# Summing softmax denominators on GpSimd instead of TensorE in a decoder's first attention

## The chip, the cores and the metric

The kernel runs on one core of one Trainium2 chip. The metric is the device time of one execution in microseconds (us), the median of several runs. Each execution computes two whole decoder layers; the change touches only the first of the stages, the attention of layer 0.

## The reference

The input x is 4 x 512 x 512, float32. What the first stage computes, per batch of 512 tokens (the rest of the two layers follows and is untouched):

```python
def rotate_half(x):
    x1, x2 = jnp.split(x, 2, axis=-1)
    return jnp.concatenate([-x2, x1], axis=-1)
q, k, v = h @ Wq.T, h @ Wk.T, h @ Wv.T          # h = layernorm(x)
q = q * cos + rotate_half(q) * sin
k = k * cos + rotate_half(k) * sin
# 16 heads of 32 features
q_feat, k_feat = jax.nn.elu(q) + 1.0, jax.nn.elu(k) + 1.0
memory = jnp.einsum('bhsd,bhse->bhde', k_feat, v)
mem_out = (q_feat @ memory) / (q_feat . k_feat.sum(over keys))
attn = softmax(q @ k.T / sqrt(32)) @ v
combined = sigmoid(gate) * mem_out + (1 - sigmoid(gate)) * attn
x = x + combined @ Wo.T
```

The softmax needs, for each head and query, a sum of exponentials over the 512 keys. Who adds them up is what changes.

## The kernel before

The stage is `attention_linear`. Its tiles bear the prefix `a_` in the profile. A batch has four chunks of four heads (QUAD), so there are 16 steps g = 0 to 15; chunk order is (0, 2, 1, 3), and c = g mod 4. Each engine runs one program written out by hand over `STEPS`, a range from g = -3 to g = 16, and each step has eight slots s = 0 to 7 (PAIRS). Slot s stands for key tile t = s // 2 (128 keys) and pair of heads w = s % 2.

In a slot TensorE does, in this order: `scores_kq(g, s)`, the transposed scores of step g (keys on partitions, L1138); `scores_qk(g + 1, s)`, the scores of the next step whose row maxima are wanted (L1120); then a half of the weighting, two slots late. `half(g, n)` is `weigh(g, t)` for even n (values times exponentials, L1150, into bank NUM) and `add_up(g, t)` for odd n (a matrix of ones times the same exponentials, L1158, into bank SUMS). Each half is four matmuls on 32 columns each of the array. So values and sums alternate, and both accumulate over the four key tiles in their banks. ScalarE turns each pair of kq banks into exponentials (L1268) in `probs`, which holds two key tiles of four heads.

Six PSUM banks rotate as three pairs, numbered by the order of `place` (the dictionary `turn`). `claim` makes TensorE wait until the pair used three places before has been drained. Hence `scores_qk(g + 1, s)` waits for the exponentials of slot s - 1, and what follows slot 7 of an even step (`values`, or `outputs`) gets the pair of kq slot 7 and waits for that slot's exponentials.

Other work rides along. In an even step the rotation of steps g + 2 and g + 3 is made: `rotate_first`, `rotate_second` and `rotate_third` on VectorE (L1387, L1390, L1394), and on GpSimd L1505 (`rot1`), L1506 (`mul3`), `low(g + 2)` (L1483) and L1510 (`rot2`). In an odd step GpSimd has `low(g + 2)` alone, and after `normalise` two `linear` (L1497). `normalise(g - 1)` (L1487 and L1492) writes `oT`, which the output product of a batch needs. At c = 2 TensorE computes `values` of the next batch at slot 0 and after slot 7; at odd steps it has the matmuls of the linear memory (L1172, L1181, L1182, L1190) and two `project` after slot 7 (L59 to L61); at c = 0 `outputs` (L1225) stands after slot 7 and needs `normalise(g - 1)`; at c = 1 it stands at slots 1, 3 and 5, each followed by VectorE's `add_residual` (L1413) and a store and a load of `res` on the SP queue. ScalarE's `maxima_rows` issues two DMAs that put the maxima beside the operands of the next step's kq scores.

The SP queue carries `stack(g)`, 12 DMAs each (L1073), and the residual's. `cosT` and `sinT` hold both rotated chunks (two of 128 rows) for the whole stage.

## Time and profile before

| | |
|---|---|
| time, median of 3 runs | 3030.02 us (3027.96 to 3043.7) |
| the profiled execution: span, first to last instruction | 3028.2 us (the median lies 1.8 us above it) |
| the stage of the change, by its instructions | about 20 us to 666 us of the span |
| PE busy, whole span | 2476.7 us (82%) |
| DVE, ACT, POOL busy, whole span | 1884.0, 1239.5, 851.9 us |
| exponentials of the stage (L1268) | 128 instructions, 130.8 us |

PE is TensorE, DVE is VectorE, ACT is ScalarE, POOL is GpSimd, SP is SyncE with its DMA queue. In the views, x counts instructions; a float32 matmul appears as two instructions, so four matmuls of a half read x8. Timelines give start, duration, engine, line, operation and tiles, and in brackets the idle time before and who ended it. PEclk is the granted TensorE clock, 1.00 for 2.4 GHz and 0.50 for 1.2 GHz.

### The profile page before, as it was taken

What the parts mean: (1) busy time and instruction counts of PE and PEld (TensorE: products, weight loads), DVE (VectorE), ACT (ScalarE), POOL (GpSimd) and SP (SyncE); (2) the same over time, 40 slices, a digit from 0 to 9 for tenths busy, and PEclk for the clock granted to TensorE, in tenths of its full rate; (3) what the DMA queues carried; (4) which work ended last, traced back from release to release, by engine and by line L of the source; (5) the groups of instructions that cost most, each with busy time, mean ns of one, the idle gap of its engine ahead of it and who ended that gap; (6) DMA issues with size and microseconds to landing.
All of it is one profiled execution on the core that took longest, in us unless ns stands there. A gap on an engine that the chain in (4) does not pass through costs nothing. (4 is left out here: it accounts for less than half of the span.)

```text
span 3028.2 us, 35090 instructions
## 1 busy us (share of the span) xinstructions
PE 2476.7 (82%) x12822; PEld 1644.7 (54%) x12822; DVE 1884.0 (62%) x2959; ACT 1239.5 (41%) x1873; POOL 851.9 (28%) x1176
## 2 busy tenths in 40 slices
PE   5898989864443357999448999999999879999999
PEld 4454545321222237998334554545555538888887
DVE  3766575627899985778557777565655444444443
ACT  2444444428656625666103433334333323333332
POOL 2232222215657634555343332001211110000000
PEclk8999999976665678999768999999999979999999
DMA  3213132212222346988585655334433423101000
GB/s 117 65 43 84 43 84 46 70 61 77 77 80 77 108 163 213 308 300 289 158 185 136 159 146 157 88 89 104 109 95 91 115 80 127 42 0 42 1 28 15
DMA packets 186940, 323.55 MB, mean 107 GB/s; under 512 B 20450, under 2 KB 52066, under 8 KB 186788
## 3 DMA queue, kind: packets, MB, share of 16 engines
q1 hardware_dynamic: 168356, 270.44, 30.0%
q0 software_dynamic: 15360, 50.34, 6.3%
q8 instruction: 88, 1.44, 0.2%
q10 hardware_dynamic: 3072, 0.79, 0.1%
q14 instruction: 64, 0.52, 0.1%
HBM read 182.30 MB, written 62.92 MB: 81 GB/s over the span
## 5 line engine op out<-in xcount | busy, mean ns | idle before, releaser
L757 DVE TENSOR_REDUCE at_negmax<-at_ps 128x2 f32<-128x1024 f32 (+3 forms) x256 | 259.1, 1016 | 120.3 <-PE at_ps L523 63.1
L670 ACT ACTIVATE at_probs<-at_ps 128x1024 f32<-128x1024 f32 (+3 forms) x256 | 221.7, 866 | 267.4 <-PE at_ps L538 263.3
L1367 DVE TENSOR_REDUCE a_negmax<-a_ps 128x2 f32<-128x1024 f32 x128 | 155.2, 1217 | 136.4 <-PE a_ps L1120 135.8
L59 PE MATMUL ff_ps<-ff_xnT_hi,ff_s_hi 128*128 128x512 f32 x512 | 200.8, 392 | 5.1 <-DVE ff_xnT_lo L2878 5.1
L60 PE MATMUL ff_ps<-ff_xnT_lo,ff_s_hi 128*128 128x512 f32 x512 | 200.1, 391 | 0.0
L61 PE MATMUL ff_ps<-ff_xnT_hi,ff_s_lo 128*128 128x512 f32 x512 | 200.1, 391 | 0.0
L1946 ACT ACTIVATE gr_act_signs<-gr_signed,gr_test 128x512 bf16<-128x512 f32 x248 | 177.4, 717 | 42.3 <-POOL gr_test L2339 20.4
L2908 DVE TENSOR_TENSOR ff_hid<-ff_hid,ff_ps 128x512 f32<-128x512 f32 x64 | 44.0, 688 | 238.6 <-ACT ff_hid L2853 238.6
L538 PE MATMUL at_ps<-at_qk 98*128 98x512 f32 (+3 forms) x512 | 171.7, 417 | 21.0 <-DMA at_qk<-at_mrow 10.6
L1268 ACT ACTIVATE a_probs<-a_ps 128x1024 f32<-128x1024 f32 x128 | 130.8, 1023 | 135.2 <-PE a_ps L1138 134.6
L518 PE MATMUL at_ps<-at_qk 96*128 96x512 f32 (+3 forms) x512 | 162.9, 382 | 19.0 <-DVE at_xnT_lo L818 8.9
L538 PEld LDWEIGHTS at_ps<-at_qk 98*128 98x128 f32 x512 | 83.3, 194 | 162.5 <-issue 93.6
L2853 ACT ACTIVATE ff_hid<-ff_ps 128x512 f32<-128x512 f32 x64 | 38.3, 598 | 303.3 <-PE ff_ps L61 303.3
L59 PE MATMUL ex_ps<-ex_x_hi,ex_gu_hi 128*128 128x256 f32 x512 | 148.4, 290 | 6.3 <-issue 5.8
L60 PE MATMUL ex_ps<-ex_x_lo,ex_gu_hi 128*128 128x256 f32 x512 | 145.7, 285 | 0.0
L61 PE MATMUL ex_ps<-ex_x_hi,ex_gu_lo 128*128 128x256 f32 x512 | 145.6, 284 | 0.0
L852 POOL TENSOR_SCALAR_AFFINE_SELECT at_probs<-at_probs 128x256 f32<-128x256 f32 x128 | 52.4, 411 | 291.4 <-ACT at_probs L670 291.4
L782 DVE RECIPROCAL at_weighed<-at_weighed 128x128 f32<-128x128 f32 x128 | 119.7, 939 | 15.2 <-ACT at_weighed L705 15.2
L2635 POOL TENSOR_TENSOR ex_d_lo<-first_d,ex_d_hi 128x1024 fp32r<-128x1024 f32 x32 | 87.4, 2730 | 136.5 <-ACT ex_d_hi L2561 136.4
L873 POOL TENSOR_TENSOR at_oT<-at_weighed 128x512 f32<-128x512 f32 x32 | 40.7, 1270 | 296.6 <-DVE at_weighed L782 296.6
L726 ACT CAST at_part<-at_ps 128x512 fp32r<-128x512 f32 x64 | 37.4, 587 | 211.7 <-PE at_ps L61 200.7
L630 PE MATMUL at_ps<-at_wo,at_oT 128*128 128x512 f32 x256 | 115.9, 607 | 6.8 <-POOL at_oT L873 6.6
(431 smaller groups left out, 6640.1 us busy)
## 6 DMA issues: line engine op xcount, KB each, us to landing
at_qk<-at_part SPq DMA_DIRECT2D x384, 128.0 KB
first_gu<-in_L_ffn_w_gate_up_dram SPq DMA_DIRECT2D x32, 1024.0 KB, 13.4
a_qk<-a_part SPq DMA_DIRECT2D x192, 128.0 KB
first_d<-in_L_ffn_w_down_dram SPq DMA_DIRECT2D x32, 512.0 KB, 13.6
out_rows<-ex_y SPq DMA_DIRECT2D x32, 512.0 KB
gr_aside_raw<-in_L_ffn_W_dram SPq DMA_DIRECT2D x48, 256.0 KB, 3.1
w13T<-gr_aside_out SPq DMA_DIRECT2D x32, 256.0 KB, 3.2
shared_x<-x_after_cross SPq DMA_DIRECT2D x8, 1024.0 KB
```

What stands on the lines that cost most here:

```text
L59: pe.matmul(out, lh, rh, start=start, stop=False, skip_group_check=True)
L60: pe.matmul(out, lh, rl, start=False, stop=False, skip_group_check=True)
L61: return pe.matmul(out, ll, rh, start=False, stop=stop, skip_group_check=True)
L518: mm = pe.matmul(bank(key, i, 0, n), qk[0:KROWS, g % STACKS, 0, j, t * P:(t + 1) * P], qk[0:KROWS, g % STACKS, 1, j, 0:n], start=True, sto ...
L538: mm = pe.matmul(bank(key, i, lo), qk[0:KROWS + 2, g % STACKS, 1, j, t * P:(t + 1) * P], qk[0:KROWS + 2, g % STACKS, 0, j, lo:S], start=Tr ...
L630: mm = pe.matmul(bank(key, i), oT[:, dc, t * P:(t + 1) * P], woT[:, dc, :], start=dc == 0, stop=dc == NC - 1, skip_group_check=True)
L670: act.activation(probs[:, t % 2, 2 * w:2 * w + 2, lo:S], banks(("kq", g, s), lo), ACT.Exp, scale=SCALE).then_inc(free(("kq", g, s)), 1)
L757: dve.reduce_max(negmax[:, g % 2, :].rearrange("p (j t) -> p j t", t=NT)[:, 2 * w:2 * w + 2, t], banks(("qk", g, s), 0, width(g, t)), AX.X ...
L782: dve.reciprocal(weighed[:, 1, t * P:(t + 1) * P], weighed[:, 1, t * P:(t + 1) * P]).then_inc(rec_done, 1)
L1268: act.activation(probs[:, t % 2, 2 * w:2 * w + 2, :], banks(("kq", g, s)), ACT.Exp, scale=SCALE).then_inc(free(("kq", g, s)), 1)
L1367: dve.reduce_max(negmax[:, g % 2, :].rearrange("p (j t) -> p j t", t=NT)[:, 2 * w:2 * w + 2, t], banks(("qk", g, s)), AX.X, negate=True).t ...
L1946: act.activation(act_signs[:, j, :], src, ACT.Sign, scale=-1.0, bias=against, accum_out=total[:, i, j:j + 1]).then_inc(counted_to[j], 1)
```

## The change

TensorE no longer runs `add_up` for each key tile. GpSimd adds the exponentials of key tiles 1, 2 and 3 onto those of tile 0, in place, with six additions of 128 x 1024 per step (`fold`, three for each pair of heads), and `add_up(g)` then runs once per step, in slot 1 of the next step. `probs` becomes five half tiles (a half is one key tile and one pair of heads, 128 x 1024): three are used in turn for w = 0, two for w = 1. Tile 0's half must now stay until the sum is taken, so for w = 1 the tiles 1, 2 and 3 all use the same half. The exponentials wait for the values' matmuls and the fold that last read their half. `cosT` and `sinT` hold one chunk each and are loaded anew in odd steps by `load_tables`, after `stack`, 256 KB a table; the gate's load gets a semaphore of its own.

```diff
-        probs = sb("probs", [P, 2, QUAD, S])
+        probs = sb("probs", [P, 5, 2, S])
-        cosT, sinT = sb("cosT", [P, NC // 2, S]), sb("sinT", [P, NC // 2, S])
+        cosT, sinT = sb("cosT", [P, 1, S]), sb("sinT", [P, 1, S])
...
+        def at_half(g, t, w):
+            if w == 0:
+                return ((0, 1, 2, 1)[t] - g) % 3
+            return 3 + (g + (t > 0)) % 2
+
+        def probs_of(g, t, j):
+            return probs[:, at_half(g, t, j // 2), j % 2, :]
+
+        def both_of(g, t, w):
+            return probs[:, at_half(g, t, w)]
...
         @block.sync
         def _(sp):
+            def load_tables(n):
+                if n:
+                    sp.wait_ge(const_in, 32 * n)
+                    sp.wait_ge(mul1, 2 * n)
+                    sp.wait_ge(mul2, n)
+                    sp.wait_ge(mul3, n)
+                for dst, src in ((cosT, env.cos), (sinT, env.sin)):
+                    sp.dma_start(dst[:], src.rearrange("(c p) s -> c p s", p=P)[n % 2].rearrange("p (o s) -> p o s", o=1)).then_inc(const_in, 16)
...
                 if has(g + 2):
                     stack(g + 2)
+                if g % 2 and g >= -1 and has(g + 3):
+                    load_tables((g + 3) // 2)
...
-            def add_up(g, t):
-                if t == 0 and g >= 1:
+            def add_up(g):
+                if g >= 1:
                     pe.wait_ge(sums_out, g)
+                for w in range(2):
+                    pe.wait_ge(folded[w], (NT - 1) * (g + 1))
                 for j in range(QUAD):
-                    mm = pe.matmul(ps[j * HD:(j + 1) * HD, SUMS, :], ones[:], probs[:, t % 2, j, :],
-                                   start=t == 0, stop=t == NT - 1, skip_group_check=True)
+                    mm = pe.matmul(ps[j * HD:(j + 1) * HD, SUMS, :], ones[:], probs_of(g, 0, j), start=True, stop=True, skip_group_check=True)
                 mm.then_inc(sums_done, 1)
 
             def half(g, n):
                 if n % 2 == 0:
                     weigh(g, n // 2)
-                else:
-                    add_up(g, n // 2)
+                elif n == PAIRS - 1:
+                    add_up(g)
...
                 act.wait_ge(kq_ready, PAIRS * g + s + 1)
-                if NT * g + t >= 2:
-                    act.wait_ge(sums_done, NT * g + t - 1)
-                act.activation(probs[:, t % 2, 2 * w:2 * w + 2, :], banks(("kq", g, s)), ACT.Exp, scale=SCALE
-                               ).then_inc(free(("kq", g, s)), 1)
+                if t == 0 and g:
+                    act.wait_ge(values_done, NT * g - (1, 0)[w])
+                    act.wait_ge(folded[w], (NT - 1) * g - (1, 0)[w])
+                if t == 1 and g:
+                    act.wait_ge(sums_done, g)
+                if t == 3 or (t, w) == (2, 1):
+                    old = t - 2 + w
+                    act.wait_ge(values_done, NT * g + old + 1)
+                    act.wait_ge(folded[w], (NT - 1) * g + old)
+                act.activation(both_of(g, t, w), banks(("kq", g, s)), ACT.Exp, scale=SCALE).then_inc(free(("kq", g, s)), 1)
...
         @block.gpsimd
         def _(pool):
+            def fold(g, t, w):
+                wait_drained(pool, "kq", g, 2 * t + w)
+                if t == 1:
+                    wait_drained(pool, "kq", g, w)
+                    pool.wait_ge(values_done, NT * g + 1)
+                else:
+                    pool.wait_ge(folded[w], (NT - 1) * g + t - 1)
+                pool.tensor_tensor(both_of(g, 0, w), both_of(g, 0, w), both_of(g, t, w), ALU.add).then_inc(folded[w], 1)
+
+            def fold_tile(g, t):
+                for w in range(2):
+                    fold(g, t, w)
...
+                own = has(g)
                 if g % 2 == 0 and has(g + 2):
                     pool.wait_ge(mul1, g + 4)
                     pool.tensor_tensor(turn1[:], turn1[:], turn2[:], ALU.subtract).then_inc(rot1, 1)
-                    pool.tensor_tensor(raw[1][:], raw[1][:], table(cosT, g + 2), ALU.mult).then_inc(mul3, 1)
+                    pool.tensor_tensor(raw[1][:], raw[1][:], table(cosT), ALU.mult).then_inc(mul3, 1)
+                    if own:
+                        fold_tile(g, 1)
                     low(g + 2)
                     pool.wait_ge(mul2, g // 2 + 2)
                     pool.wait_ge(mul3, g // 2 + 2)
                     pool.tensor_tensor(raw[1][:], raw[1][:], turn2[:], ALU.add).then_inc(rot2, 1)
-                if g % 2 and has(g + 2):
+                elif g % 2 and has(g + 2):
                     low(g + 2)
+                    if own:
+                        fold_tile(g, 1)
+                elif own:
+                    fold_tile(g, 1)
+                if own:
+                    fold_tile(g, 2)
+                    fold_tile(g, 3)
                 if has(g - 1):
                     normalise(g - 1)
```

The order on GpSimd in an even step with rotation (here g = 2), before: L1505 and L1506 are `rot1` and `mul3`, L1483 is `low`, L1510 `rot2`, L1487 and L1492 `normalise(g - 1)`, and then comes `low` of step 3.

```order
L1505 TENSOR_TENSOR a_turn<-a_turn 128x1024
L1506 TENSOR_TENSOR a_raw<-a_raw,a_cosT 128x1024
L1483 TENSOR_TENSOR a_part<-a_turn,a_part 128x2x512
L1510 TENSOR_TENSOR a_raw<-a_raw,a_turn 128x1024
L1487 TENSOR_TENSOR a_weighed<-a_weighed 128x512
L1492 TENSOR_TENSOR a_oT<-a_weighed,a_lin 128x512
```

The same place in the changed kernel (L1547, L1548, L1524, L1554, L1528 and L1533 are the same operations, L1516 is a fold):

```order
L1547 TENSOR_TENSOR a_turn<-a_turn 128x1024
L1548 TENSOR_TENSOR a_raw<-a_raw,a_cosT 128x1024
L1516 TENSOR_TENSOR a_probs<-a_probs 128x1024 x2
L1524 TENSOR_TENSOR a_part<-a_turn,a_part 128x2x512
L1554 TENSOR_TENSOR a_raw<-a_raw,a_turn 128x1024
L1516 TENSOR_TENSOR a_probs<-a_probs 128x1024 x4
L1528 TENSOR_TENSOR a_weighed<-a_weighed 128x512
L1533 TENSOR_TENSOR a_oT<-a_weighed,a_lin 128x512
```

Two folds now stand ahead of `low`, four between `rot2` and `normalise`.

ScalarE over the slots 4 to 7 of an even step of the changed kernel (g = 0), with the semaphores that each instruction waits on (L1297 is the exponentials, L1313 and L1318 belong to the feature map, L1327 are the DMAs of the maxima):

```order
L1297 ACTIVATE a_probs<-a_ps 128x1024 [waits a0_kq_ready]
L1313 ACTIVATE a_raw<-a_turn 128x1024 [waits a0_mul2,a0_rot1]
L1297 ACTIVATE a_probs<-a_ps 128x1024 [waits a0_folded1,a0_values_done,a0_kq_ready]
L1318 ACTIVATE a_turn<-a_turn 128x1024 [waits a0_feat_exp,a0_p_lo]
L1297 ACTIVATE a_probs<-a_ps 128x1024 [waits a0_folded0,a0_values_done,a0_kq_ready]
L1297 ACTIVATE a_probs<-a_ps 128x1024 [waits a0_folded1,a0_values_done,a0_kq_ready]
L1327 DMA a_qk<-a_mrow 1x16x128 [waits a0_w_turned]
```

Before, each of these exponentials waited on `sums_done` and `kq_ready`; those of slots 5, 6 and 7 now wait on folds and on the values' matmuls.

## Rows read from the trace of the kernel before

**Rows 1.** Busy time, steps 2 to 5: stretch, length, PE, PEld, DVE, ACT, POOL, PEclk, DMA.

```profile
165.70:194.64 28.94, 28.42 (x147) 15.51 (x145) 19.48 (x18) 15.29 (x16) 11.80 (x6) 1.00 0.24 56
194.64:231.87 37.23, 36.32 (x194) 21.65 (x193) 22.39 (x27) 16.34 (x20) 8.67 (x6) 1.00 0.19 44
231.87:260.23 28.36, 23.03 (x107) 8.74 (x105) 23.12 (x31) 14.25 (x15) 14.80 (x7) 0.88 0.38 103
260.23:313.37 53.14, 49.74 (x235) 27.82 (x234) 30.66 (x37) 17.25 (x21) 7.47 (x5) 1.00 0.24 65
```

**Rows 2.** Timeline of PE, step 6: in slots 1 and 2, then at its end.

```profile
322.02 1.07 PE L1158 MATMUL a_ps<-a_probs,a_ones 128*32 128x512 f32 x8
323.02 0.73 PE L1138 MATMUL a_ps<-a_qk 98*128 98x512 f32 x2
...
336.72 0.28 PE L1127 MATMUL a_ps<-ident,a_negmax 128*16 128x128 f32 x1 [0.33 <-DVE a_negmax L1367]
342.34 0.62 PE L1138 MATMUL a_ps<-a_qk 98*128 98x512 f32 x2
```

**Rows 3.** Timeline of POOL, step 6.

```profile
324.57 2.37 POOL L1505 TENSOR_TENSOR a_turn<-a_turn 128x1024 f32<-128x1024 f32 x1 [16.87 <-DVE a_turn L1390]
326.89 2.39 POOL L1506 TENSOR_TENSOR a_raw<-a_raw,a_cosT 128x1024 f32<-128x1024 f32 x1
329.24 3.37 POOL L1483 TENSOR_TENSOR a_part<-a_turn,a_part 128x1024 fp32r<-128x1024 f32 x1
332.57 2.38 POOL L1510 TENSOR_TENSOR a_raw<-a_raw,a_turn 128x1024 f32<-128x1024 f32 x1
```

**Rows 4.** Timeline of ACT, step 6: the exponentials of slot 7.

```profile
334.92 1.02 ACT L1268 ACTIVATE a_probs<-a_ps 128x1024 f32<-128x1024 f32 x1 [0.31 <-PE a_ps L1138]
```

**Rows 5.** Timeline of DVE, step 6: the second and the third rotation product.

```profile
323.27 1.22 DVE L1390 TENSOR_TENSOR a_turn<-a_raw,a_sinT 128x1024 f32<-128x1024 f32 x1
...
327.53 2.84 DVE L1394 TENSOR_TENSOR a_turn<-a_raw,a_sinT 128x1024 f32<-128x1024 f32 x1
```

**Rows 6.** Busy PE in stretches around the end of step 0: PEclk, DMA.

```profile
118.00:120.00 2.00, 0.00 (x0) 0.85 0.87 199
120.00:122.00 2.00, 1.28 (x3) 0.50 0.59 133
...
126.00:128.00 2.00, 2.00 (x13) 0.95 0.00 0
```

**Rows 7.** Timeline of POOL, step 4: its first row and its `normalise`.

```profile
237.71 2.38 POOL L1505 TENSOR_TENSOR a_turn<-a_turn 128x1024 f32<-128x1024 f32 x1 [11.53 <-DVE a_turn L1390]
...
251.39 1.26 POOL L1487 TENSOR_TENSOR a_weighed<-a_weighed 128x512 f32<-128x512 f32 x1 [3.28 <-DVE a_weighed L1380]
252.73 2.13 POOL L1492 TENSOR_TENSOR a_oT<-a_weighed,a_lin 128x512 f32<-128x512 f32 x1
```

**Rows 8.** Timeline of PE at the end of step 4: the output product.

```profile
254.91 5.88 PE L1225 MATMUL a_ps<-a_wo,a_oT 128*128 128x512 f32 x8 [4.12 <-POOL a_oT L1492]
```

**Rows 9.** Timeline of POOL, step 0: its first row.

```profile
104.19 2.38 POOL L1505 TENSOR_TENSOR a_turn<-a_turn 128x1024 f32<-128x1024 f32 x1 [10.44 <-DVE a_turn L1390]
```

**Rows 10.** Timeline of PE: first matmul of step 1.

```profile
120.21 1.22 PE L1138 MATMUL a_ps<-a_qk 98*128 98x512 f32 x2 [3.61 <-DMA a_qk<-a_mrow]
```

**Rows 11.** Timeline of ACT, step 15: the maxima's DMAs, the exponentials of slot 2.

```profile
616.05 1.15 ACTq L1299 DMA_DIRECT2D a_qk<-a_mrow  x2
...
625.31 1.02 ACT L1268 ACTIVATE a_probs<-a_ps 128x1024 f32<-128x1024 f32 x1
```

**Rows 12.** Timeline of PE, step 15: its first matmul, the last product with ones.

```profile
618.51 1.22 PE L1138 MATMUL a_ps<-a_qk 98*128 98x512 f32 x2 [3.46 <-DMA a_qk<-a_mrow]
...
635.57 1.04 PE L1158 MATMUL a_ps<-a_probs,a_ones 128*32 128x512 f32 x8
```

**Rows 13.** Timeline of SP's queue, step 5: one `stack`.

```profile
266.87 8.45 SPq L1073 DMA_DIRECT2D a_qk<-a_part  x12
```

**Rows 14.** Timeline of DVE, step 5: a residual addition.

```profile
280.56 0.69 DVE L1413 TENSOR_TENSOR a_res<-a_ps,a_res 128x512 f32<-128x512 f32 x1 [2.47 <-DMA a_res<-in_x_dram]
```

More of the change, by code:

```diff
@@ L981, in linear_unit, with table @@
             return m if g % 2 and s >= first and (s - first) % 3 == 0 and has(m) else None
-        def table(which, m):
-            c = chunk(m)
-            return which[:, c:c + 1, :].to_broadcast([P, 2, S])
+        def table(which):
+            return which[:].to_broadcast([P, 2, S])
+        def at_half(g, t, w):
[6 more added lines that the diff above has]
+            return probs[:, at_half(g, t, w)]
         def reciprocal_parts(g, s):
@@ L1040, in attention_linear @@
         stack_in, mx_in = [sem(f"stack_in{i}") for i in range(STACKS)], sem("mx_in")
-        res_in, res_out, const_in = sem("res_in"), sem("res_out"), sem("const_in")
+        res_in, res_out, gate_in, const_in = sem("res_in"), sem("res_out"), sem("gate_in"), sem("const_in")
+        folded = [sem(f"folded{w}") for w in range(2)]
         ones_set, rows_set, gates = sem("ones_set"), sem("rows_set"), sem("gates")
@@ L1061, in _ @@
         def _(sp):
[L1062 to L1064 removed]
+            def load_tables(n):
[6 more added lines that the diff above has]
+                    sp.dma_start(dst[:], src.rearrange("(c p) s -> c p s", p=P)[n % 2].rearrange("p (o s) -> p o s", o=1)).then_inc(const_in, 16)
+            load_tables(0)
+            sp.dma_start(gate_e[:], gate.rearrange("a h b c -> (a b c h)").partition_broadcast(P)).then_inc(gate_in, 16)
             def stack(g):
@@ L1382, in rotate_first @@
             def rotate_first(m):
-                dve.wait_ge(const_in, 16 * 3)
+                dve.wait_ge(const_in, 32 * (m // 2 + 1))
                 wait_drained(dve, "p", m + 1)
```

15 lines of the change are left out of this document (6 added, 9 removed).

## The prediction

> **What bounds the kernel now.** I read the stage step by step, since the share of busy time over the whole span says nothing of it. The busy time of the steps [rows 1] shows TensorE working 28.42 of 28.94 us in step 2, 36.32 of 37.23 in step 3 and 49.74 of 53.14 in step 5, and GpSimd 7 to 15 us in any of them. Only step 4 leaves TensorE idle, 5.3 us of 28.36. So work taken off TensorE is worth its full time here, as long as nothing else becomes late, and GpSimd has room on average. The average is not what decides. The timelines of single engines show when GpSimd's work falls due: in step 6 four operations stand back to back from 324.57 to 334.95 [rows 3], and the exponentials of slot 7 start at 334.92 [rows 4]. GpSimd is full in the very part of an even step in which the folds are wanted.
>
> **Removed: TensorE.** One half of products with ones lasts 1.00 us from its start to the next matmul's (322.02 to 323.02, [rows 2]). There were four a step, one is left: 3 x 16 = 48 go, 48 us at most. In the seven odd steps 1 to 13 I count 3.0 us each, 21 us, because their slots are spread by the linear memory's matmuls and the output products, so GpSimd's `low` and six folds (7 x 2.35 = 16.5 us of a step of 37 or 53 us, [rows 1]) find room. In the even steps the gain lies under a longer chain on another engine, and I count nothing for it.
>
> **Added: six folds a step.** A fold is 128 x 1024 float32 with two inputs and an output in SBUF, as L1505 and L1506 are; these follow each other at 2.32 and 2.35 us [rows 3]. I take 2.35. A TensorE slot took about 2.1 us and would now take less, so folds are slower than slots even with nothing else on GpSimd.
>
> For w = 1 the tiles 1, 2 and 3 share one half tile, so the exponentials of slot 5 wait for fold (1, 1), and those of slot 7 for fold (2, 1). In GpSimd's order, slot 7's exponentials of an even step stand behind `rot1`, `mul3`, two folds, `low`, `rot2`, two folds. From the start of L1505 that is 2.32 + 7 x 2.35 = 18.8 us, plus what the two engines cost each other: `low` takes 3.33 us instead of 2.35 where VectorE's L1394 runs beside it [rows 3, 5], so 1.0 for that one, and I put 1.0 more for the feature map's addition at the end of the step, which has two SBUF inputs too. Sum 20.8 us. Today L1505 to the exponentials is 334.92 - 324.57 = 10.35 us. L1505 itself waits on VectorE's second product in slot 1, which nothing moves. **Slot 7 is 10.4 us late in an even step**, and its three saved halves lie inside this wait.
>
> What waits for it. **Steps 2, 6, 10:** `values` after slot 7 claims the PSUM pair of that very slot. Today it runs right behind the maxima's transpose, 336.72 to 342.34, 5.6 us [rows 2]. Now: 324.57 + 20.8 + 1.0 = 346.4, plus 5.6 gives 352.0, 9.6 later than 342.34. TensorE will have idled 4 to 5 us before. At the end of step 0 such an idle stretch of 3.6 us took the granted clock from 1.00 to 0.50, and it stayed there for some 6 us from 120 on [rows 6, 10]; matmuls then take twice as long, so 3.0 us of work are lost. 12.6 us each, 37.8 together. **Steps 4, 8, 12:** `outputs` needs `normalise(g - 1)`, which now stands behind all six folds. From L1505 at 237.71 [rows 7]: 20.8 + two folds 4.7 + L1487 and L1492, which take 254.91 - 251.39 = 3.5 today with a collision and 2.7 without (I take 3.0), gives 266.2 against 254.91 [rows 8], 11.3 each, 33.9 together. The clock is already at half there: eight matmuls take 5.88 us; no more is lost. **Step 0** has no `outputs`: the maxima's DMAs stand behind slot 7 on ScalarE, and the next matmul comes 2.46 us after their issue [rows 11, 12]. 104.19 + 20.8 + 1.0 + 2.5 = 128.5 against 120.21 [rows 9, 10], 8.3 us. The even steps cost 80.0 us.
>
> **Steps 14 and 15.** Step 14 has no rotation: folds from the end of slot 2's exponentials reach slot 7 where it is now, no change. In step 15 slots are short (no next scores), and nothing hides the last folds: slot 2's exponentials end at 626.3 [rows 11], six folds end at 640.4, and the sum's matmuls start there instead of at 635.57 [rows 12]. +4.9 us.
>
> **Tables.** Two DMAs more on the SP queue behind `stack`. 12 DMAs take 8.45 us to issue [rows 13], so 1.4 us, and 512 KB to move. Only in steps 5 and 9 does something urgent stand behind them, the residual's store and load, on which VectorE already waits 2.47 us [rows 14]. Bounds 0 and 5 us; I take 3, nearest to the issue time twice. The smaller first load is hidden by the projections and gives nothing. `outputs` of slots 3 and 5 and the PSUM pairs behind them would be late next.
>
> **Sum:** -21 + 80.0 + 4.9 + 3 = +67 us. 3028.2 + 67 = 3095.2 for the profiled execution; the median lies 1.8 above its span, so **3097 us**. Bounds: without the lower clock in steps 2, 6, 10 (-9), without the second collision (-7) and with tables free (-3) it is 3078. A collision more for each of two folds in each even step (+14) and odd steps that keep a third of their gain (+14) make 3125.
>
> One rule to set beside this. The Trainium skill, page "SBUF — State Buffer", section "SBUF: two separate sides", says that VectorE instructions with two SBUF inputs and GpSimd instructions take a shared pair of ports as an exclusive lock, and the loser waits out the whole instruction. Here the trace agrees: L1394, alone worth 1.22 us, takes 2.84 and ends 1.1 us after L1506 [rows 3, 5]. By that rule the price of folds is not GpSimd's alone; it is rival 2.
>
> **Rivals.**
> 1. *TensorE keeps its gain* (the other side: faster). Place: slots 5 to 7 of even steps. If the exponentials don't in fact meet unfinished folds, all 48 us come off: 2982. It decides at a lateness of (21 - 5 - 3) / 7 = 1.9 us per even step: below it the kernel is faster. For it: over steps 2 and 3 together GpSimd's 20.5 us [rows 1] and twelve folds (28.2 us) fill 49 of 66 us. Against: its own four operations fill the 10.35 us before slot 7 already, so four folds would have to take under 0.5 us each.
> 2. *The ports spread the delay.* VectorE's rotation, feature and layernorm operations in odd steps meet folds too, each 1.6 us longer, as L1394 is [rows 5]. With four such meetings in an odd step and two thirds of them on the path of the maxima, 7 x 4 x 1.1 = 31 us more than forecast: 3128. For: folds fill 14 of 37 us. Against: VectorE is busy 22 to 31 us of 37 to 53 in those steps and has room.
> 3. *Later work absorbs part.* The step after a late slot 7 finds its operands, tables and maxima long ready, and runs closer together; half of the lateness comes back: 3055.
> 4. *Nothing measurable,* if lateness and gain cancel: 3035. Against: they differ by a factor of four.
>
> **How the numbers follow.** Forecast 0.64, rival 2 (or odd steps bound by folds) 0.14, rival 3 0.14, rival 4 0.04, rival 1 0.04. The range 3055 to 3128 takes in forecast, its bounds, and the edges of rivals 2 and 3, and leaves out some 0.18. The measurement can tell about 0.5%, 15 us. Below 3015: 0.04; within: 0.05; above 3045: 0.91.
>
> **What would show it.** L1505's counterpart to the exponentials of slot 7 should be about 20.8 us in steps 2, 4, 6; ScalarE should wait on GpSimd's folds there, which no row shows today. TensorE's wait before `values` 4 to 5 us, before `outputs` some 11 more than 4.12, PEclk 0.5 after both. Step 3's stretch should be 3 us shorter, less what the clock takes. If the span between L1505 and slot 7 stays near 10 us, the folds' order or their cost is misread, and the sum falls with it; if odd steps are not shorter, rival 2 holds.

## The result and the profile after

The changed kernel takes 3116.93 us (median of 4 runs, 3108.18 to 3120.89) beside 3030.3 us (3027.96 to 3043.7) for the kernel before on the same chip: ratio 1.0272, 95% interval 1.0245 to 1.0298. The profiled span is 3116.2 us against 3028.2, 88 us longer. The forecast was 3097, in a range of 3055 to 3128. The direction and most of the mechanism were right, but one term of the sum, the gain in odd steps, fell altogether: it was 21 us off, and the range held the result in part because the even steps came out 7 us cheaper than forecast.

GpSimd is busy 1081.7 us over the whole span (851.9 before), TensorE 2461.5 (2476.7). The folds' group (L1516):

```profile
L1516 POOL TENSOR_TENSOR a_probs<-a_probs 128x1024 f32<-128x1024 f32 x96 | 241.8, 2541 | 104.5 <-ACT a_probs L1297 75.0
```

The 96 folds take 2541 ns each on average, where I had 2350. Steps 2 to 5 in windows, columns as in [rows 1] (stretch, length, PE, PEld, DVE, ACT, POOL, PEclk, DMA share, GB/s):

```profile
174.00:213.85 39.85, 29.85 (x123) 17.50 (x121) 20.29 (x18) 15.30 (x16) 27.73 (x12) 0.83 0.18 41
213.85:250.70 36.85, 33.95 (x171) 21.06 (x170) 24.02 (x27) 16.37 (x20) 22.46 (x11) 1.00 0.23 58
250.70:289.97 39.27, 22.15 (x82) 9.00 (x81) 23.09 (x31) 14.34 (x15) 28.62 (x13) 0.74 0.28 74
289.97:345.34 55.37, 48.19 (x212) 27.92 (x211) 34.15 (x37) 17.25 (x21) 21.51 (x11) 0.97 0.26 72
```

Against [rows 1], step 2 is 10.9 us longer, step 4 the same 10.9, step 3 0.4 shorter, and step 5 2.2 longer. GpSimd now works 27.7 of 39.9 us in step 2, where it worked 11.8 of 28.9. TensorE does less: 2.4 us less in step 3 and 1.6 less in step 5. It waits more: (36.85 - 33.95) - (37.23 - 36.32) = 2.0 us more in step 3 and (55.37 - 48.19) - (53.14 - 49.74) = 3.8 us more in step 5.

**The chain before slot 7, step 6.** GpSimd's timeline (start, length, engine, line and operation; in brackets the idle time before and what ended it) and below it ScalarE's exponentials of slot 5 and slot 7:

```profile
356.53 2.38 POOL L1547 TENSOR_TENSOR a_turn<-a_turn 128x1024 f32<-128x1024 f32 x1 [13.85 <-DVE a_turn L1418]
358.87 2.39 POOL L1548 TENSOR_TENSOR a_raw<-a_raw,a_cosT 128x1024 f32<-128x1024 f32 x1
361.22 5.63 POOL L1516 TENSOR_TENSOR a_probs<-a_probs 128x1024 f32<-128x1024 f32 x2
366.82 2.34 POOL L1524 TENSOR_TENSOR a_part<-a_turn,a_part 128x1024 fp32r<-128x1024 f32 x1
369.13 2.36 POOL L1554 TENSOR_TENSOR a_raw<-a_raw,a_turn 128x1024 f32<-128x1024 f32 x1
371.46 10.28 POOL L1516 TENSOR_TENSOR a_probs<-a_probs 128x1024 f32<-128x1024 f32 x4
```

```profile
366.97 1.02 ACT L1297 ACTIVATE a_probs<-a_ps 128x1024 f32<-128x1024 f32 x1 [3.48 <-POOL a_probs L1516]
...
376.21 1.02 ACT L1297 ACTIVATE a_probs<-a_ps 128x1024 f32<-128x1024 f32 x1 [5.05 <-POOL a_probs L1516]
```

The first row answers to L1505 of [rows 3]. From it to slot 7's exponentials pass 376.21 - 356.53 = 19.7 us, and 10.35 before: 9.3 us late, forecast 10.4. GpSimd does not rest in between. The two bracketed waits for a fold are of a kind that no row of before has. Over the whole stage (60 to 750 us) the waits read (us in total, times, longest):

```profile
ACT a_probs L1297 <- POOL a_probs L1516: 70.1, 18, 5.1
PE a_ps L1247 <- POOL a_oT L1533: 37.1, 4, 9.9
ACT a_lin L1368 <- POOL a_oT L1533: 36.5, 7, 5.4
```

**The clock.** TensorE in stretches of 2 us around these waits (length, busy, PEclk, DMA share, GB/s):

```profile
362.00:364.00 2.00, 0.47 (x2) 1.00 0.00 0
364.00:366.00 2.00, 0.26 (x2) 0.63 0.00 0
366.00:368.00 2.00, 0.00 (x0) 0.50 0.00 0
...
378.00:380.00 2.00, 2.00 (x6) 0.50 0.75 168
380.00:382.00 2.00, 2.00 (x7) 0.60 0.00 0
```

TensorE works 0.73 us in the six from 362 to 368, and the granted clock falls from 1.00 to 0.50, the 1.2 GHz level. It is still there in the fully busy stretch behind slot 7 and only begins to rise in the one after it. TensorE's two long waits are at the second matmul group of slot 6 and at the first matmul of `values`:

```profile
368.05 1.22 PE L1141 MATMUL a_ps<-a_qk 96*128 96x512 f32 x2 [3.78 <-ACT a_probs L1297]
...
377.29 0.80 PE L59 MATMUL a_ps<-a_wv_hi,a_xnT_hi 128*128 128x512 f32 x1 [2.45 <-ACT a_probs L1297]
```

The wait at which the clock falls is the one for slot 5's exponentials; the wait before `values` is 2.45 us, where I had 4 to 5. Two terms add up to what step 6 costs. Counted from GpSimd's first row of the step, `values` starts after 377.29 - 356.53 = 20.76 us, and before after 336.75 - 324.57 = 12.18: 8.6 later. From its first matmul to the next step's first kq matmul pass 384.88 - 377.29 = 7.59 us, before 342.34 - 336.75 = 5.59: 2.0 more at the lower clock. Together 10.6 us. Steps 2 and 10 read 8.6 and 2.3, 8.6 and 2.5. Ahead of slot 7's exponentials the lower clock adds nothing, since these end by waiting 5.05 us for a fold.

**The whole stage in a table.** I cut it at two marks of TensorE's timeline: a step's first kq matmul, and the next maxima's transpose (L1148, before L1127). "Slots" is from the first to the second, "boundary" from there to the next step's first kq matmul. Each number is after less before, in us.

```
step       0     1     2     3     4     5     6     7     8     9    10    11    12    13    14
slots    +5.2  +2.2  +5.3  -0.4  +5.0  +2.2  +5.8  -0.5  +4.9  +2.0  +5.5  -0.4  +5.1  -1.8  -1.0
boundary +1.6   0.0  +5.6   0.0  +5.9   0.0  +4.8  +0.1  +6.4   0.0  +5.5   0.0  +6.2  +3.2   0.0
```

Even steps 0 to 12 cost 36.8 in their slots and 36.0 at their boundaries; odd steps cost 3.3; step 14 gives 1.0 and the boundary before it takes 3.2; step 15 costs 6.3, and the stage begins 0.6 earlier. That makes the 84.0 us by which the last product with ones is later (719.57 against 635.57, [rows 12]). The remaining 4 us of the span lie behind this stage, in code that the change doesn't touch; the same stretch takes between 2389 and 2401 us in the profiled executions of all the kernels here, so 4 us of it mean nothing.

### The profile page after: what moved, and what is told of

It is laid out like the page before. It is cut to its first block and busy times, and to the rows that moved or that the text cites. A ratio compares the mean times of both kernels' runs of the same rounds, so it can differ in the third digit from the quotient of the medians.

```text
span 3116.2 us, 34542 instructions
## 1 busy us (share of the span) xinstructions
PE 2461.5 (79%) x12438; PEld 1649.4 (53%) x12438; DVE 1910.3 (61%) x2959; ACT 1240.1 (40%) x1873; POOL 1081.7 (35%) x1272
## 5 line engine op out<-in xcount | busy, mean ns | idle before, releaser
L1516 POOL TENSOR_TENSOR a_probs<-a_probs 128x1024 f32<-128x1024 f32 x96 | 241.8, 2541 | 104.5 <-ACT a_probs L1297 75.0
L1395 DVE TENSOR_REDUCE a_negmax<-a_ps 128x2 f32<-128x1024 f32 x128 | 155.5, 1219 | 160.9 <-PE a_ps L1141 160.7
L1297 ACT ACTIVATE a_probs<-a_ps 128x1024 f32<-128x1024 f32 x128 | 130.2, 1024 | 205.5 <-PE a_ps L1159 135.1
L1141 PE MATMUL a_ps<-a_qk 96*128 96x512 f32 x256 | 92.0, 446 | 52.3 <-ACT a_probs L1297 30.9
```

What stands on the lines that cost most here:

```text
L1297: act.activation(both_of(g, t, w), banks(("kq", g, s)), ACT.Exp, scale=SCALE).then_inc(free(("kq", g, s)), 1)
L1395: dve.reduce_max(negmax[:, g % 2, :].rearrange("p (j t) -> p j t", t=NT)[:, 2 * w:2 * w + 2, t], banks(("qk", g, s)), AX.X, negate=True).t ...
L1516: pool.tensor_tensor(both_of(g, 0, w), both_of(g, 0, w), both_of(g, t, w), ALU.add).then_inc(folded[w], 1)
```

## The experiments

All ratios are to the kernel before, timed on the same chip. Tables "slots" and "boundary" are cut as above, each less the kernel before. Where folds are kept in some steps only, the code says so by one function, and the other steps let TensorE sum each tile with ones as before:

```
def folds(g): return g % 2 == 1          # odd_fold; == 0 in even_fold
...
-                elif n == PAIRS - 1:
-                    add_up(g)
+                elif n == PAIRS - 1 or not folds(g):
+                    add_up(g, n // 2)
```

Half tiles are then given out by a table (the one that comes free first), and the exponentials wait for its last readers.

### tables_only: the tables per chunk, without a fold

```
(the kernel before)
-        cosT, sinT = sb("cosT", [P, NC // 2, S]), sb("sinT", [P, NC // 2, S])
+        cosT, sinT = sb("cosT", [P, 1, S]), sb("sinT", [P, 1, S])
...
                 if has(g + 2):
                     stack(g + 2)
+                if g % 2 and g >= -1 and has(g + 3):
+                    load_tables((g + 3) // 2)
```

> The kernel before, with only the tables changed: one chunk each, loaded anew in odd steps behind the stack's DMAs. The sums stay with TensorE. My term: the tables cost 3 us in all (0 to 5), so 3033 against 3030. Rival: the tables are what made steps 5 and 9 of the changed kernel 8.2 and 8.3 us longer where the other odd steps grew by 3.8 to 5.1; then they cost 4 to 5 us in each of the two, 8 to 10 us in all, 3039, and VectorE's wait for the residual's load in step 5 grows from 2.47 us to over 4.

Measured: 3042.18 us against 3031.18, 1.0030 (1.0015 to 1.0045): some 9 us by the ratio, 11 by the medians, so the rival was right and my 3 us were a third of it. (One of its twelve executions took 13225 us and is left out of the ratio.) The step table places 9.0 us in the slots of steps 5 (+5.2) and 9 (+3.8), as the prediction did; the profiled stage also begins 2.0 us later and its step 3 is 0.7 longer, which stays unexplained. SP's queue there, with the tables' two DMAs ahead of the residual's store and load, then VectorE's addition that needs the load, then the matmuls of the linear memory (L1190 before), which need the PSUM pair that this addition frees:

```profile
277.85 0.47 SPq L1068 DMA_DIRECT2D a_cosT<-in_cos_dram  x1
278.36 0.45 SPq L1068 DMA_DIRECT2D a_sinT<-in_sin_dram  x1
278.85 0.43 SPq L1090 DMA_DIRECT2D x_after_attn<-a_res  x1
...
282.61 0.33 SPq L1086 DMA_DIRECT2D a_res<-in_x_dram  x1
...
285.24 0.69 DVE L1422 TENSOR_TENSOR a_res<-a_ps,a_res 128x512 f32<-128x512 f32 x1 [4.78 <-DMA a_res<-in_x_dram]
...
286.08 3.75 PE L1199 MATMUL a_ps<-a_turn 128*128 128x512 f32 x4 [3.67 <-DVE a_res L1422]
```

The same places of the kernel before:

```profile
275.36 0.59 SPq L1083 DMA_DIRECT2D x_after_attn<-a_res  x1
...
277.79 0.33 SPq L1079 DMA_DIRECT2D a_res<-in_x_dram  x1
...
281.40 1.95 PE L1190 MATMUL a_ps<-a_turn 128*128 128x512 f32 x4 [1.36 <-DVE a_res L1413]
```

From store to load pass 3.76 us instead of 2.43, and the two issues ahead of the store take 1.0 us: about half of the delay is the queue's issue time, about half the longer way from store to load. The load waits for the store's end; that the store is slower because 512 KB of tables move at the same time is my reading, which no run separates. VectorE waits 4.78 us instead of 2.47 [rows 14] and TensorE 3.67 instead of 1.36, after which the same four matmuls last 3.75 us instead of 1.95. TensorE's clock in tables_only around that wait:

```profile
282.00:284.00 2.00, 0.41 (x2) 1.00 0.14 37
284.00:286.00 2.00, 0.00 (x0) 0.81 0.27 101
286.00:288.00 2.00, 1.92 (x3) 0.50 0.35 131
288.00:290.00 2.00, 2.00 (x7) 0.50 0.43 125
290.00:292.00 2.00, 2.00 (x9) 0.50 0.02 6
```

The 2.3 us of waiting were in my bounds; the six microseconds at half clock behind them, in which 3 us of work are lost, were not. Together they are the 5.2 us of step 5. In the kernel before, the granted clock stays at 1.00 there.

### late_tables: the same loads behind the residual's store and load

```
-                if g % 2 and g >= -1 and has(g + 3):
-                    load_tables((g + 3) // 2)
                 if c == 1 and b >= 1:
                     store(b - 1, 1)
                     load_residual(b - 1, 2)
                     ...
                     store(b - 1, 3)
+                if g % 2 and g >= -1 and has(g + 3):
+                    load_tables((g + 3) // 2)
```

> The changed kernel with the tables' loads moved behind the residual's stores and loads of the same step. If the tables delay the residual, 6 to 10 us come back (3117 to 3107 to 3111), all of it in steps 5 and 9. If my term was right (3 us), 3114, inside the spread of the runs. Nothing at all if the residual waits for the 12 stack DMAs and not for the tables.

Measured: 3113.53 against 3031.18, 1.0270 (1.0246 to 1.0293). Steps 5 and 9 now cost +0.2 and -1.5 in place of +2.2 and +2.0, but step 1 costs +4.3 in place of +2.2. Of the 3.4 us gained by the medians nothing is certain: the intervals of this kernel and of the change overlap almost wholly. The place of the tables' cost is shown: 5.5 us of it come back in steps 5 and 9. Step 1's 2.1 us are the clock's. TensorE's waits within it are the same or shorter (the longest 2.77 us, and 2.78 in the change), but the granted clock is 0.80 over the step instead of 0.86, and TensorE is busy 44.20 us instead of 41.86. Why the clock differs at equal waits stays open.

### odd_fold and even_fold: which steps pay

> Folds only in odd steps; in even steps TensorE adds up tile by tile as before. Forecast's terms: 21 us of gain in odd steps 1 to 13, 4.9 lost in step 15, 3 for tables: 3030 - 13 = 3017. Rival 2 (folds and VectorE's operations with two SBUF inputs hold each other up): odd steps gain only about 0.5 us each, as step 7 of the changed kernel did, so 3030 - 4 + 5 + 3 to 9 for tables = 3034 to 3040.

Measured: 3050.86 against 3031.18, 1.0069 (1.0045 to 1.0092). Slots of the odd steps: +1.8, -0.5, +1.5, -0.5, +2.0, +2.7, -1.8; boundary before step 14 +3.2; step 15 +3.8. Even steps are within 0.3 in their slots. So folding where GpSimd has most room is slower too, and the number lies outside both expectations. Where the gain went is seen in step 7. VectorE's addition for the feature map, and the qk matmul (a score for the next step's maxima) that TensorE was kept from:

```profile
359.66 2.94 DVE L1457 SCALAR_TENSOR_TENSOR a_raw<-a_raw 128x1024 f32<-128x1024 f32 x1
```

```profile
364.59 0.73 PE L1174 MATMUL a_ps<-a_qk 96*128 96x512 f32 x2 [1.08 <-DVE a_negmax L1425]
```

Before, that addition takes 1.22 us:

```profile
354.34 1.22 DVE L1399 SCALAR_TENSOR_TENSOR a_raw<-a_raw 128x1024 f32<-128x1024 f32 x1
```

In the changed kernel as a whole, by tile shape, the eight of them (L1427 there) and the same line before:

```profile
L1427 DVE SCALAR_TENSOR_TENSOR a_raw<-a_raw 128x1024 f32<-128x1024 f32 x8 | 21.7, 2712 | 0.0
```

```profile
L1399 DVE SCALAR_TENSOR_TENSOR a_raw<-a_raw 128x1024 f32<-128x1024 f32 x8 | 9.7, 1215 | 0.0
```

Not everything in the odd steps' numbers comes from GpSimd or VectorE. Steps 7 and 11 of odd_fold do the same work and have the same waits of TensorE (0.92, 1.08 or 1.07, and 0.68 us), but step 11 is 3.1 us longer, at a lower granted clock (columns as in [rows 1]):

```profile
347.66:384.46 36.80, 33.90 (x170) 21.03 (x169) 24.03 (x27) 16.37 (x20) 23.63 (x12) 1.00 0.23 59
...
497.12:537.06 39.94, 37.06 (x170) 23.27 (x169) 24.02 (x27) 16.38 (x20) 23.68 (x12) 0.91 0.24 60
```

> Folds only in even steps; odd steps as before. The chain on GpSimd makes steps 0, 4, 8, 12 about 8 to 11 us longer and 2, 6, 10 about 10.6 (from the changed kernel's trace: 17.77 to 28.35 us between the first rotation operation and the next step's first matmul in step 6), 72 us together, plus 3 to 9 for the tables: 3105 to 3111. If the odd steps of the changed kernel also suffer from the lateness of the even ones and not from their own folds, this kernel keeps that loss too and comes out at 3117.

Measured: 3107.3 against 3031.18, 1.0245 (1.0223 to 1.0267), as expected. Slots of even steps +5.1 to +5.8, boundaries +4.2 to +5.7, as in the change (step 0: +1.0). The two halves of the change add up within the intervals: 19.7 + 76.1 = 96 us over before for both, where the change itself is 87 over; the 9 us between them fit the tables, which both kernels carry: even_fold's steps 5 and 9 cost +5.2 and +3.9 in their slots without a fold, as in tables_only.

### half_fold: GpSimd's chain shortened

```
-                pool.tensor_tensor(both_of(g, 0, w), both_of(g, 0, w), both_of(g, t, w), ALU.add).then_inc(folded[w], 1)
+                pool.tensor_tensor(both_of(g, 0, w)[:, 0], both_of(g, 0, w)[:, 0], both_of(g, t, w)[:, 0], ALU.add).then_inc(folded[w], 1)
```

> The changed kernel with each fold adding only the first head of its pair (128 x 512, some 1.28 us instead of 2.35), so the sums of the second heads leave out the key tiles 1 to 3. The waits and their order are the same. If the chain on GpSimd sets the even steps, each fold in it gives back 1.07 us: four in steps 0, 2, 6, 10 (4.3 us each) and six in 4, 8, 12 (6.4 each), 36 us, and 3 to 6 more in steps 14 and 15: 3117 to about 3077. If the folds' number and the waits cost the time and not their length, it stays near 3117.

Measured, one run: 3060.79 us, beside 3033.92. Six folds of half the size, and 56 us of the 87 are gone, without one wait or instruction less. Step 6 again:

```profile
339.51 2.38 POOL L1547 TENSOR_TENSOR a_turn<-a_turn 128x1024 f32<-128x1024 f32 x1 [14.96 <-DVE a_turn L1418]
...
344.20 3.48 POOL L1516 TENSOR_TENSOR a_probs<-a_probs 128x512 f32<-128x512 f32 x2
...
352.27 4.97 POOL L1516 TENSOR_TENSOR a_probs<-a_probs 128x512 f32<-128x512 f32 x4
```

```profile
354.88 1.02 ACT L1297 ACTIVATE a_probs<-a_ps 128x1024 f32<-128x1024 f32 x1 [2.89 <-POOL a_probs L1516]
```

The chain takes 15.4 us instead of 19.7, and the exponentials still end by waiting for a fold (2.89 us). Boundaries of steps 2 to 12 fall from 4.8 to 6.4 each to 0.4 to 3.4 each, slots from about 5.3 to 3.0 to 3.6. The time follows the length of GpSimd's queue; this is the strongest evidence for the chain. The even steps give back 12.7 us in their slots and 25.0 at their boundaries, 37.7 where I expected 36. That this one execution came out 16 us below my number has other causes. Odd steps give back 6.5 us in their slots, where VectorE's feature addition reads 1.85 us in the middle instead of 2.92, step 15 gives 7.4, step 14 and the boundary before it 1.6, and some 5 us are the stretch behind the stage, which varies by as much in any case.

### norm_early: `normalise` ahead of the last folds

```
+                early = own and has(g - 1) and (c == 0 or g == G - 3)
                     ...
                     fold_tile(g, 2)
+                if early:
+                    normalise(g - 1)
+                if own:
                     fold_tile(g, 3)
-                if has(g - 1):
+                if has(g - 1) and not early:
                     normalise(g - 1)
```

> The changed kernel with normalise of the step before put ahead of the last tile's two folds on GpSimd, in steps 4, 8, 12 (and 13). If the output product of steps 4, 8, 12 waits on normalise behind six folds, it comes forward by some 5.4 us in each, until slot 7's exponentials hold it (16 us), and the 3.2 us before step 14 come back too: 3117 to about 3098. Rival: the delay is set by slot 7's exponentials alone; then nothing moves.

Measured: 3102.79 against 3033.92, 1.0230 (1.0215 to 1.0246), 13 to 14 us of the 19 that I expected. The boundaries of steps 4, 8 and 12 fall from +5.9, +6.4, +6.2 to +1.9, +0.7, +2.2, and the one before step 14 from +3.2 to +0.9: 16.0 us of boundaries. Step 8's GpSimd and the output product:

```profile
439.52 4.66 POOL L1516 TENSOR_TENSOR a_probs<-a_probs 128x1024 f32<-128x1024 f32 x2
444.14 2.25 POOL L1528 TENSOR_TENSOR a_weighed<-a_weighed 128x512 f32<-128x512 f32 x1
446.46 1.26 POOL L1533 TENSOR_TENSOR a_oT<-a_weighed,a_lin 128x512 f32<-128x512 f32 x1
447.69 4.64 POOL L1516 TENSOR_TENSOR a_probs<-a_probs 128x1024 f32<-128x1024 f32 x2
```

```profile
447.78 5.11 PE L1247 MATMUL a_ps<-a_wo,a_oT 128*128 128x512 f32 x8 [5.12 <-POOL a_oT L1533]
```

In the changed kernel TensorE waits 9.85 us at that product, here 5.12. In steps 4, 8 and 12 the product starts 27.8 us after GpSimd's first row of the step in the change, 17.2 before and 23.2 here. So 4.6 of its 10.6 us of lateness are the position of one pair of instructions in a queue; the slots of these steps are unchanged (+4.9, +5.0, +4.8), because slot 7 stands where it stood.

### even_split: half of the folds on VectorE, in even steps

```
+        def on_vector(g, t, w):
+            return g % 2 == 0 and w == 1
...
(VectorE, behind the maxima of a slot)
+                    for h, t, w in ((g, (s - 1) // 2, (s - 1) % 2), (g - 1, (s + 7) // 2, (s + 7) % 2)):
+                        if has(h) and 1 <= t < NT and folds(h) and on_vector(h, t, w):
+                            fold(dve, h, t, w)
...
(GpSimd)
+                    if not on_vector(g, t, w):
+                        fold(pool, g, t, w)
```

> The changed kernel with the folds of the second pair (w = 1) done by VectorE in even steps. GpSimd's chain before slot 7 then has no fold of its own pair, and slot 7 waits for VectorE's fold (2, 1). If the chain of GpSimd sets the even steps' loss (72.8 us of slots and boundaries), two folds less before slot 7 and three less before normalise bring back at least 4.7 us in each of steps 0, 2, 6, 10 and 7.1 in 4, 8, 12: 40 us, and more where VectorE's own wait is shorter; 3060 to 3077. If VectorE, which meets GpSimd at the ports, becomes the bound, less than 20 us come back.

Measured: 3104.3 against 3033.92, 1.0233 (1.0216 to 1.0249). A miss: under 20 us back, as the rival said. Boundaries of even steps do shrink, from 36.0 to 13.1 us. Slots of even steps stay at +3.9 to +4.6, now with ScalarE's exponentials waiting for VectorE's folds (33.5 us in 16 waits), and slots of odd steps rise to +3.8, +3.6, +3.9, +3.6, +2.0, +0.4. The folds' line on VectorE over the stage (fastest/median/slowest ns, then the stretch):

```profile
L1100 DVE TENSOR_TENSOR a_probs<-a_probs x24: 1149/2020/2518, 110.7 to 682.6; 128x1024 f32<-128x1024 f32 x24
```

The same addition takes 1149 ns at best and 2020 in the middle. The work was moved from an engine that had a queue to one that feeds TensorE in every slot. How much of the loss is VectorE's added work and how much the lengthened rows, this run does not tell.

The Trainium skill, page "SBUF — State Buffer", section "SBUF: two separate sides", describes how two such operations meet: the ports that the two engines share are taken as a lock, and the other waits until a whole instruction is over. The rows of step 7 of odd_fold agree: a fold starts at 359.16, the feature addition at 359.66, and a whole fold and a whole addition one behind the other, 359.16 + 2.35 + 1.22, would end at 362.73, where the addition ends at 362.60. The runs show the lengthened rows, not the lock itself.

### odd_wait: a fold held back until the feature addition is done

```
(odd_fold)
                 for w in range(2):
+                    if g % 2 and has(g + 2) and (t, w) == (1, 1):
+                        pool.wait_ge(feat_done, g + 3)
                     fold(g, t, w)
```

> Folds only in odd steps (3050.9), and GpSimd waits for VectorE's feature addition before fold (1, 1) of an odd step. Step 7 showed that addition take 2.94 us beside a fold instead of 1.22, and TensorE then wait for a PSUM pair from VectorE. If this meeting eats the gain, steps 3, 7, 11 become 1 to 2 us shorter each, and 1, 5, 9 not longer: about 3045. If VectorE is simply full there, nothing changes (3051), or the later folds make it slower.

Measured: 3041.59 against 3033.92, 1.0032 (1.0019 to 1.0045), 0.37 points of the ratio, some 11 us, better than odd_fold (9 us by the medians). It adds a wait on GpSimd and is faster. In step 7:

```profile
352.87 1.22 DVE L1457 SCALAR_TENSOR_TENSOR a_raw<-a_raw 128x1024 f32<-128x1024 f32 x1
```

```profile
354.16 7.02 POOL L1100 TENSOR_TENSOR a_probs<-a_probs 128x1024 f32<-128x1024 f32 x3 [3.83 <-DVE a_raw L1457]
```

The addition is back at 1.22 us, and odd slots read -2.7, -1.8, +0.9, -1.8, +2.0, -1.5, -1.8 in place of +1.8, -0.5, +1.5, -0.5, +2.0, +2.7, -1.8. Steps 5 and 9, the tables' steps, are the two that stay positive. The collision is therefore a cause: all eight additions of this kind are back at 1212 to 1217 ns, with nothing else in the program changed.

Its price is less sure. The two tables differ by 11.9 us, but the profiled execution of odd_wait, 3030.92 us, is the fastest of its six (the others took 3038 to 3045). In steps 3 and 7, at a granted clock of 1.00 in both kernels, the wait gave 1.3 us each, and 0.6 and 0 in steps 5 and 9. The 4.5 us of step 1 and the 4.2 of step 11 hold some 3 us each of a higher clock: step 11 of odd_fold is the slow one shown above, and in odd_late step 1 has the waits of odd_wait (1.28 us for the maxima in place of 2.78), a clock of 0.87 as in odd_fold, and gains 1.5 us. So 6 us are the collision's by rows at equal clock; 9 to 11 by the times of all executions.

### odd_four and all_four: the tables loaded once, four half tiles

A half tile takes 4 KB of each partition, as much as the second chunks of both tables. Here one half tile gives way to them:

```
-        probs = sb("probs", [P, 5, 2, S])
+        probs = sb("probs", [P, 4, 2, S])
-        cosT, sinT = sb("cosT", [P, 1, S]), sb("sinT", [P, 1, S])
+        cosT, sinT = sb("cosT", [P, NC // 2, S]), sb("sinT", [P, NC // 2, S])
```

odd_four keeps the wait of odd_wait and folds in steps 1 to 13 (step 13 too, which its expectation left out); all_four folds everywhere.

> Folds in the odd steps 1 to 11 alone, with GpSimd's wait for the feature addition, and four half tiles instead of five, so that both chunks' tables fit and are loaded once as before. What the runs leave of the gain: 2.7, 1.8, 1.8 and 1.5 us in steps 1, 3, 7, 11, up to 3 in each of 5 and 9 now that no table stands before the residual, and no loss in steps 13 and 15: 10 to 14 us, 3017 to 3021 against 3031, just past what can be told from no change. If the four half tiles make ScalarE wait for folds in odd steps, nothing is left (3031 or more).

> The changed kernel's folds in all steps, with four half tiles and the tables loaded once. If the tables cost the 9 us that they cost the kernel before, it comes to 3108; if only the 3 us that came back with the late tables, 3114. One condition differs: for w = 0 too the tiles 1 to 3 share a half, so slot 4 waits for fold (1, 0) and slot 6 for fold (2, 0); both end before slot 5's and 7's folds do, and should cost nothing.

Measured: odd_four 3049.56 against 3032.11, 1.0066 (1.0043 to 1.0088); all_four 3133.25, 1.0346 (1.0320 to 1.0373). all_four lies outside what I expected; odd_four falls under the alternative that nothing is left. Odd slots of odd_four read -2.0, +0.4, -1.1, +0.4, -0.1, +0.5, +2.2: steps 5 and 9 are better than odd_wait's by 2.0 and 2.1, and 3, 7, 11 worse by 2.0 to 2.2. ScalarE never waits for a fold in it, as the expectation had feared, but for the values' matmuls that still read the half (3.89 us at one place of step 3), and TensorE then waits 1.19 and 0.53 us for exponentials, which it doesn't in odd_wait. Even slots of all_four cost +8.8 in place of 5.2, their boundaries 15.4 in all in place of 36.0: 77.3 us together in place of 72.6. The fifth half tile is thus worth some 2 us in steps 3, 7 and 11, and these two runs do not tell the tables' price apart from it. They are inconclusive for what they were made for.

### mended: the three repairs in the changed kernel

norm_early, the wait of odd_wait and late_tables together, with all folds.

> The changed kernel with three places mended together: normalise ahead of the last folds (gave 14 us), the feature addition before fold (1, 1) in odd steps (gave 9 in the kernel with odd folds), late tables (3). If they are separate costs, 26 us come back, 3091, and what is left, some 60 us, is slot 7's wait in even steps, which none of them touches. If they overlap, 3098 to 3103.

Measured: 3089.88 against 3032.11, 1.0197 (1.0173 to 1.0222): 27 us better than the change, as expected for separate costs. By the tables 17.5 us come back at the boundaries and 11.9 in the slots of odd steps. These read -0.7, -1.8, +0.2, -1.8, -1.6, -1.8, -1.0. What is left is mostly the chain: even slots +5.2 to +5.7, boundaries of steps 2, 6, 10 +5.6 each, and ScalarE's wait for folds, 70.3 us in 18 waits, where the changed kernel has 70.1 in 18.

### odd_late: folds where nothing waits for them

```
+        def folds(g):
+            return g % 2 == 1 and g < 12
```

with the wait of odd_wait and late_tables.

> The last attempt at a version that keeps a gain: folds in the steps 1, 3, 5, 7, 9, 11 alone, five half tiles, GpSimd's wait for the feature addition, tables loaded behind the residual's. From the step tables: 2.7 + 3 x 1.8 us of gain in 1, 3, 7, 11, 2 to 3 in each of 5 and 9, nothing lost in 13 and 15: 12 to 14 us, 3018 against 3031. If the tables' loads cost something even there, or TensorE is held in those steps by VectorE, less than 6 us are left, which can't be told from no change.

Measured: 3022.62 against 3033.27, 0.9969 (0.9956 to 0.9981): 11 us faster than the kernel before, and the fastest of all. Slots of odd steps 1 to 11 read +0.3, -1.8, -2.5, -1.8, -1.8, -1.9, and no boundary or tail costs anything above 0.7. Step 3 in the windows (columns as above) shows what a clean odd step yields:

```profile
195.91:231.37 35.46, 33.64 (x170) 21.13 (x169) 22.34 (x27) 16.25 (x20) 22.67 (x12) 1.00 0.24 61
```

TensorE works 33.64 us where it worked 36.32 [rows 1], 2.7 less and not 3.0, and the step is only 37.23 - 35.46 = 1.8 shorter. The rest has become idle time (1.8 us instead of 0.9), and the timeline names who is awaited. The wait shown is there before too (0.91 us); new are one of 0.69 us at the next features and one of 0.19 for exponentials, all for ScalarE:

```profile
203.75 0.49 PE L1238 MATMUL a_ps<-a_v,a_turn 128*128 128x128 f32 x2 [0.92 <-ACT a_turn L1392]
```

## Why the prediction held, and where it failed

Term by term, in us:

| term | forecast | measured |
|---|---|---|
| L1505's counterpart to slot 7's exponentials (10.35 before) | 20.8 | 19.7 |
| step 0 | +8.3 | +6.8 |
| steps 2, 6, 10 | +37.8 | +32.5 |
| steps 4, 8, 12 | +33.9 | +33.5 |
| odd steps, tables in them included | -21 + 3 = -18 | +3.3 |
| step 14 and the boundary before it | 0 | -1.0 + 3.2 |
| step 15 | +4.9 | +6.3 |
| sum in the stage (start -0.6, rest +0.1) | +67 | +84 |

- **Slot 7 late in even steps: right.** Folds stand in GpSimd's order ahead of `low` and `rot2`, and the exponentials of slots 5 and 7 wait for folds. half_fold halved the folds and got 56 us back; even_fold kept the cost with folds in even steps alone. The chain was 1.1 us shorter than I had, since only one collision shows in it (two folds in 5.63 us instead of 4.7), where I had put two. From GpSimd's first row to slot 7's exponentials pass 19.6 to 19.7 us in all seven even steps.
- **The lower clock in steps 2, 6, 10: there, and smaller.** `values` starts 8.6 us later (forecast 9.6) and takes 2.0 to 2.5 longer (forecast 3.0), 10.8 a step where I had 12.6. The clock falls earlier than I had it, since slot 5's exponentials wait too and TensorE is idle there first (3.78 us); what it costs ahead of slot 7's exponentials is hidden under their own wait. All even steps together come to 72.8 us against 80.0.
- **`outputs` in steps 4, 8, 12: right in size (33.5 against 33.9).** The product starts 10.6 us later (forecast 11.3), and 0.3 to 0.7 more are lost behind it, where I counted nothing. norm_early cut TensorE's wait there from 9.85 to 5.12 us.
- **The step that failed: "In the seven odd steps 1 to 13 I count 3.0 us each, 21 us, because [...] GpSimd's `low` and six folds [...] find room".** They found room on GpSimd, and that was not the question. Three things ate the gain. First, VectorE's feature addition takes 2.94 us instead of 1.22 beside a fold; VectorE has no slack there (in step 7 of odd_fold it is busy all the time from 359 to 367 us), and the maxima come late (a qk matmul waits 1.09 us for L1395 in the change). odd_wait took this collision away alone and was faster for it, by 1.3 us in each of steps 3 and 7 and by 6 to 11 in all. That is rival 2's mechanism. I dismissed it because VectorE "is busy 22 to 31 us of 37 to 53": again an average over a step, the very thing the first paragraph warned of. Second, the tables cost 9 us in the kernel before and not 3; in the change itself moving them gave 5.5 back in steps 5 and 9. Third, even a clean odd step yields 1.8 us, not 3.0: TensorE's work is 2.7 less, and it then waits 0.9 us longer for ScalarE. For steps 3 and 7 this closes the account: 1.8 of clean gain, less 1.3 for the collision, is the 0.4 to 0.5 measured. Step 1 (+2.2) has in addition a lower clock than before, 0.86 against 0.90.
- **Tables: right place, wrong size.** I chose 3 of a range of 0 to 5. The wait grew by 2.3 us in step 5, and two such steps are within the bounds; the slower matmuls behind it (3.75 us for 1.95) were not counted, although I had counted just that for steps 2, 6 and 10.
- **Step 14: not foreseen.** ScalarE's scaling of `lin` (L1368) waits for `o_done`, that is for `normalise(g - 1)` behind six folds:

```profile
414.71 0.69 ACT L1368 ACTIVATE a_lin<-a_ps,a_g_sig 128x512 f32<-128x512 f32 x1 [5.37 <-POOL a_oT L1533]
```

It happens in all seven odd steps (the 36.5 us of the waits above). In six of them TensorE's projections hide it. Behind step 13 there are none, and the maxima's DMAs stand behind L1368 on ScalarE. norm_early brought 3.2 down to 0.9.
- **Step 15: right,** 6.3 for 4.9. The sum's matmuls wait for the last fold and run at half clock: eight take 1.94 us, 1.04 in [rows 12].

```profile
719.57 1.94 PE L1181 MATMUL a_ps<-a_probs,a_ones 128*32 128x512 f32 x8 [1.62 <-POOL a_probs L1516]
```

**Rivals.** Rival 1, the gain kept, falls: it was to decide at a lateness of 1.9 us per even step, and the lateness was 9.3. Rival 2 is half right: its mechanism is there, its price was too high: odd_wait won back 1.3 us in a step at full clock, 1.7 at most on average, where I had put 4.4 below the forecast's gain. Rival 3, that later work absorbs half, does not show: step 3 is 0.4 us shorter, not 5. Rival 4 falls with rival 1.

**Still open.** Why the granted clock falls in one step and not in another with the same waits (step 1 of late_tables, step 11 of odd_fold); what the collision costs beyond 6 us in seven odd steps; the tables' price apart from the fifth half tile in the full kernel.

## What to carry to other kernels

Before work is moved to an engine with idle time, write down its queue for the stretch in which the moved work falls due, and ask of each of its instructions who waits for the last one: here folds of 2.5 us took at most 48 us off TensorE and put 73 us on the path in seven even steps. An engine that shares a memory with another does not add to its load alone. Look at what the other does in the same microseconds, and, if the two must meet, one wait that sets them one behind the other can be worth more than it costs. And where the clock can halve, compare two kernels step by step with the clock beside each step: one profiled execution can show 3 us a step that the change did not make. Keep the move only in the steps where nobody waits: the same folds in six of sixteen steps gave a kernel 0.3% faster than before, while all sixteen gave one 2.7% slower.

## What the runs showed of the hardware

- A VectorE operation with two inputs in SBUF, 128 x 1024 float32, is not lengthened by a fixed share beside GpSimd: single rows of the feature addition read 1.22 or 2.94 us, and the folds on VectorE 1.15 to 2.52. GpSimd pays less: its folds are 2.54 us on average in the change, single ones 2.34.
- TensorE's wait of 1.36 us in step 5 left the granted clock at 1.00, one of 3.67 us at the same place came with 0.50 for some 6 us (tables_only): 2.3 us more of waiting went with 5.2 of loss.
- Equal waits do not fix the clock: steps 7 and 11 of odd_fold, both with waits of 0.9, 1.1 and 0.7 us, had a mean granted clock of 1.00 and 0.91 and took 36.80 and 39.94 us.
- 512 KB queued ahead of a store and a dependent load on the same queue stretched the time from store to load from 2.43 to 3.76 us, though both DMAs were issued in 1.0 us.
